# Neighbour maximum and graph attention on one core: the transposes of a step placed behind its second pick

## What is computed

```python
h = jnp.maximum(_layernorm(x), 0.0)
x = x + neighbour_max(h, adj)        # out[i, d] = max over j with adj[i, j] != 0 of h[j, d]
h = jnp.maximum(_layernorm(x), 0.0)
x = x + graph_attention(h, adj, W, a)  # masked softmax of leaky_relu(h W a1 + (h W a2)^T), times h W, elu
```

## Time and profile before

| | us |
|---|---|
| median of 3 runs | 768.66 (766.46 to 770.1) |
| the profiled execution | 767.11 |
| its span | 765.1 |
| TensorE busy | 699.9 (91%) |
| VectorE busy | 697.8 (91%) |
| ScalarE busy | 465.2 (61%) |
| GpSimd busy | 276.4 (36%) |

### The profile page before, as it was taken

How to read it: one execution, slowest core, us unless ns; L and a number is a source line. 1 busy time by engine, 2 the same in 40 slices (tenths; PEclk the granted TensorE clock), 3 DMA queues, 4 the chain that set the end, 5 groups by cost and what they waited for, 6 DMA issues and landing times.

```text
span 765.1 us, 14870 instructions
## 1 busy us (share of the span) xinstructions
PE 699.9 (91%) x5592; PEld 489.5 (64%) x5592; DVE 697.8 (91%) x1097; ACT 465.2 (61%) x682; POOL 276.4 (36%) x258
## 2 busy tenths in 40 slices
PE   1888999999999999999999999789999999999995
PEld 1344555555545555555555554489999999999995
DVE  9899889999999999999999999998998899899894
ACT  2878898888888889889889888363423121011000
POOL 0612033543543543543444534442330095043040
PEclk9999999999999999999999999899999999999998
DMA  9999768997777777877877754524433444543400
GB/s 306 305 372 383 278 220 270 281 309 265 254 238 253 264 232 249 274 234 239 273 244 231 274 167 147 183 84 131 132 132 111 165 141 176 179 147 143 175 20 17
DMA packets 62857, 162.55 MB, mean 212 GB/s; under 512 B 6400, under 2 KB 11136, under 8 KB 58688
## 3 DMA queue, kind: packets, MB, share of 16 engines
q1 hardware_dynamic: 53776, 138.75, 52.3%
q0 software_dynamic: 9008, 22.82, 11.0%
HBM read 117.51 MB, written 44.04 MB: 211 GB/s over the span
## 4 chain that ended last, share of the span: by engine, by line
PE 52%; ACT 18%; DVE 16%; issue 12%; DMA 1%; ACTq 0%; DVEq 0%; SPq 0%
PE pick_ps L702 22%; PE pick_ps L602 13%; ACT rest L401 7%; ACT depth L393 7%; DVE rest L1033 6%; DVE acc L855 5%; PE late_ps L574 5%; PE late_ps L615 4%; ACT edge_t L381 4%; PE order_ps L583 3%; PE late_ps L611 2%; PE late_ps L681 1%; DMA best<-x 1%; DVE acc L962 1%; PE late_ps L702 1%
## 5 line engine op out<-in xcount | busy, mean ns | idle before, releaser
L855 DVE TENSOR_TENSOR acc<-pick_ps,acc 128x1024 f32<-128x1024 f32 x248 | 302.5, 1220 | 32.9 <-PE pick_ps L602 30.4
L353 POOL DMA_INDIRECT found<-subset_max,entry x192 | 200.4, 1044 | 287.5 <-DVE entry L867 203.7
L1033 DVE SCALAR_TENSOR_TENSOR rest<-depth,curves_sb,stage 128x512 f32<-128x512 f32 x256 | 199.6, 820 | 14.7 <-PE pick_ps L702 2.3
L702 PE MATMUL pick_ps<-keys,rest 128*128 128x129 f32 x1792 | 207.1, 276 | 3.8 <-DVE rest L1033 3.8
L702 PEld LDWEIGHTS pick_ps<-keys,rest 128*128 128x128 f32 x1792 | 203.9, 192 | 7.9 <-DVE rest L1033 6.3
L392 ACT ACTIVATE first<-order_ps 128x1024 f16<-128x1024 f32 x128 | 132.4, 1035 | 64.2 <-PE order_ps L583 63.9
L393 ACT ACTIVATE depth<-order_ps 128x1024 f16<-128x1024 f32 x128 | 132.6, 1036 | 0.0
L574 PEld LDWEIGHTS late_ps<-ident_h,stage 128*128 128x128 f16 x1024 | 64.7, 100 | 84.5 <-ACT edge_t L381 53.0
L574 PE MATMUL late_ps<-ident_h,stage 128*128 128x128 f16 x1024 | 81.3, 224 | 37.5 <-ACT edge_t L381 24.4
L602 PE MATMUL pick_ps<-first,h_hi 128*128 128x512 f16 x256 | 97.8, 382 | 7.7 <-DVE acc L855 7.7
L602 PE MATMUL pick_ps<-second,h_hi 128*128 128x512 f16 x256 | 98.0, 383 | 2.3 <-DVE acc L855 2.3
(11 more groups left out here) (142 smaller groups left out, 682.0 us busy)
## 6 DMA issues: line engine op xcount, KB each, us to landing
stage<-adj SPq DMA_DIRECT2D x64, 1024.0 KB, 5.7
edge_units<-edge_t SPq DMA_DIRECT2D x64, 512.0 KB, 6.1
stage<-edge_units SPq DMA_DIRECT2D x32, 1024.0 KB, 4.8
subset_max<-keys POOLq DMA_DIRECT2D x12, 512.0 KB, 8.2
found<-subset_max,entry POOLq DMA_INDIRECT x192, 5.3
best<-x SPq DMA_DIRECT2D x4, 512.0 KB, 6.1
subset_max<-x POOLq DMA_DIRECT2D x4, 512.0 KB, 7.5
out<-keys POOLq DMA_DIRECT2D x7, 256.0 KB, 3.3
```

The costliest lines, as they stand in the source:

```text
L353: nc.gpsimd.indirect_dma_start(found[:, n % NG, s, :], None, subset_max, bass.IndirectOffsetOnAxis(entry[:, n, s:s + 1], 0)).then_inc(gath ...
L702: last = nc.tensor.matmul(out_ps(q, b), weight[:, n % WEIGHTS, b * P:(b + 1) * P], wh[:, c, :], start=c == 0 and starts(q, b), stop=c == C ...
L855: V.tensor_tensor(acc[:, q % 2, :], pick_ps[k][:, :], acc[:, q % 2, :], ALU.max).then_inc(raised, 1)
L1033: V.scalar_tensor_tensor(out=weight[:, n % WEIGHTS, :], in0=limit[:, q % 4, :], scalar=slope[:, c:c + 1], in1=units[:, m % EDGES, k * TI:( ...
```

## The change

In the queue of TensorE `flip(g + AHEAD)` moves from the place behind `rank(g + 3)` to the one behind `pick(g, 1)`, ahead of `digest`. No instruction, wait or count is added or removed, and no other queue is edited. In the last steps (from `g` = 123) there is no `flip`, and nothing differs.

```diff
@@ -715,8 +715,6 @@
                     pick(g, 0)
                     if g + 3 < PAIRS:
                         rank(g + 3)
-                    if g + AHEAD < PAIRS:
-                        flip(g + AHEAD)
                     if g == PAIRS - 4:
...
                     pick(g, 1)
+                    if g + AHEAD < PAIRS:
+                        flip(g + AHEAD)
                     if g >= 2:
                         digest(g // 2 - 1, g % 2)
```

## The result

| | before | after |
|---|---|---|
| median, us (range) | 769.38 (766.46 to 770.88) | 759.62 (758.07 to 760.85) |
| profiled execution (span) | 767.11 (765.1) | 758.9 (756.9) |
| TensorE, VectorE busy | 699.9, 697.8 | 698.5, 700.1 |

The ratio is 0.9877, with a 95% interval from 0.984 to 0.9914: the change saves 9.8 us. (The median of before is of four runs; the forecast started from three, 768.7.) The forecast was 741.7, a saving of 27, with a range of 736 to 756. The sign is right, the size is not, and 759.6 lies above the range.

What follows compares the result with a forecast made beforehand. The prediction took the turns' wait for the edge copy to bound the loop, with VectorE bounding it afterwards. Gains of 2.6, 23.0 and 1.7 us, less 0.3, gave 27.0: from the median of 768.7 to 741.7, range 736 to 756.

Steps and rivals of the forecast that it cites:

- What bounds the kernel: In the loop over `g`, dependencies closing every two steps, 7.11 us, through the wait of `flip` for the edge copy.
- the pick's leaving the loop: The second pick's four matmuls (0.86 us) leave the loop between edge copy and ranks; 6.25 us remain for two steps.
- the sum: Gains of 2.6 us (first five turns), 23.0 (other 49) and 1.7 (step 0), less 0.3 for handoffs: 27.0.
- Rival A: In the loop, VectorE sets the length after the change: 741.7 us, with 737 to 748; chance 76%.
- VectorE takes over at 53.06 to 53.15 for 16 steps: In the steady loop VectorE's own work sets the length, where 16 steps took 56.91 us; gain about 3.76.
- Step 0: VectorE's wait of 2.01 us for the second pick behind the turns goes, some 0.3 comes back: 1.7 gained.
- Bias matmul (C): The digest's bias matmul, waiting for ScalarE's key copy, inherits the turns' stall; only step 0 gains: 767 us; chance 6%.
- small matmuls (D): On TensorE, turns into digest, sixteen small matmuls in a run cost 0.34 us a step: 774 us; chance 6%.
- Rival B: A second loop of handoffs takes over; edge copy waits for turns or ScalarE's rank waits grow: 756 us; chance 12%.
- SyncE's and GpSimd's queues: Load and store come within 0.9 us of before, traffic rises to 264 GB/s, fetches keep 3 us cover: nothing lost.

## Why the prediction was wrong, step by step

**What bounds the kernel, and the pick's leaving the loop: right.** The 55 waits at the turns are gone, and the 0.86 of the second pick no longer stands between edge copy and ranks. With the fetches out of both kernels the change is worth 766.84 - 741.76 = 25.1 us; the sum said 27.0. (Rival A's low end is a slip: 768.7 - 31.0 is 737.7, not 737. Nothing hangs on it.)

**VectorE takes over at 53.06 to 53.15 for 16 steps: right but for a small term.** Without fetches it is 53.57 on average. Two takes directly behind each other cost 2.55 - 1.22 = 1.33 from start to start (the double rows at 388.58 and 389.34), as the second needs the first's `acc`. I had let a stop of 1.08 vanish to nothing; 0.11 of it stays. Four times 0.11 is 0.44 in 16 steps, which brings 53.06 to 53.50. Over 6.1 times 16 steps that is 2.7 us, enough for the difference of 25.1 and 27.0.

**Step 0: right in kind.** The changed kernel's second take follows the mask without a wait, and the next tile's first take comes at 89.00 instead of 90.15, 1.15 earlier where 1.7 was forecast:

```profile
28.85 1.44 DVE L844 TENSOR_SCALAR rest<-depth 128x2048 f16<-128x2048 f16 x1
30.21 1.22 DVE L855 TENSOR_TENSOR acc<-pick_ps,acc 128x1024 f32<-128x1024 f32 x1
```

**Bias matmul (C) and small matmuls (D): both rightly set aside.** The bias matmul at 389.30 stands 0.55 behind the turns of 388.75, where an undisturbed run of eight takes 0.45, and the waits view has no wait of it for the key copy. Turns and digest take 0.45 each (385.70, 386.15, 386.60), 0.056 a matmul, the second eight no slower than the first. The 81 ns that the Trainium skill (TensorE: Matmul & The Clock Gate, Back-to-back issue gap) gives for a lasting stream don't show in a run of sixteen.

**Rival B named a time near the result (756), but not its mechanism.** Of its signs neither came: from 60 to 490 us ScalarE's waits for ranks fell from 55.9 us to 44.4, and without fetches to 31.6, near the 0.5 a turn that was forecast, and its edge copy waits for turns once, 0.3 us. Without fetches all of the lateness went.

**SyncE's and GpSimd's queues: here the prediction failed.** I wrote that load and store "come within 0.9 us of where they were", that the traffic of 264 GB/s was under 379 shown elsewhere, and of the fetches "nothing lost". Each was costed alone: the load by its landing, the fetch by its cover, the traffic by its mean. None was held against the other. Those 0.9 us put the load behind the first fetch instead of beside it. The price was 17.9 - 2.5 = 15.4 us. It appears in a row that has no DMA in it: VectorE waiting for picks, 15.4 us against 1.6 without fetches. That 13.8 is most of the 17.9; the rest I didn't place. Over the changed-order kernels the order of their times follows these waits closely: 1.6 us at 741.8, 5.7 at 746.1, 9.5 to 10.7 at 752 to 754, 15.4 at 759.6, 18.1 at 762.3, 21.5 to 21.6 at 763.6 to 765.7 (an exception is 5.5 at 753.3). The GB/s behind the loads don't order the times so.

**What stays open.** That the fetches, by where they stand against the loads, make TensorE's signals late is shown by taking them away, by moving them and by bringing the meeting into the kernel before. How a DMA holds up TensorE's signals is not: whether it is the packets, or GpSimd's work of issuing them, no run here parts. The issuing alone is not enough, as the kernel before issues the same 192 fetches without one late signal until its loads move. Nor does the distance to the last fetch tell all: with the load one step later, loads 0.2 to 0.3 us behind a fetch had 230 to 279 GB/s, in the kernel before loads 0.05 behind one 332 to 366; and the kernel with the load one step later was the slowest of the changed order at a middling 274 GB/s.

## What to carry to other kernels

When an edit moves the wait that releases a DMA, lay the new issue time against those of the other DMA queues, fetches by index above all, and not only against the buffer that it fills: here a shift of 0.9 us went with a loss of 15.4 of 25.1 us of gain. If an engine waits for a producer whose own starts are on time, look at the DMA traffic of that moment before blaming the order of instructions. And try the order of a tight loop once with the side traffic taken out: the difference says whether to tune the loop or the traffic, and here moving six fetches by one or two takes gave back 13.5 of 17.9 us.

## What the runs showed of the hardware

- A matmul's signal can reach its waiters 0.9 us late while the starts on TensorE stay on time (pick at 386.60 to 387.24, take at 388.58 instead of 387.67), to ScalarE as to VectorE: the ranks of 370.25 released `first` at 371.45, 1.20 later, while in the kernel before it was 0.63 (ranks at 314.52, `first` at 315.15). Rows of the changed kernel, TensorE and ScalarE:

```profile
370.25 0.59 PE L583 MATMUL order_ps<-edge_t,order_w 128*128 128x512 f16 x2
```

```profile
371.45 1.02 ACT L392 ACTIVATE first<-order_ps 128x1024 f16<-128x1024 f32 x1 [1.20 <-PE order_ps L583]
```

- Only TensorE's signals were late. In the changed kernel, from 100 to 440 us, 109 of its 446 recorded ones came over 0.1 us late, of VectorE's and ScalarE's none of 599, and a take lasts 1.22 us as before. Every trace with late signals also lacks some records, so these counts are low bounds.
- From 1.5 to 5 us behind a load of 1 MB that was issued 0.3 to 1.2 us behind an indirect fetch of 128 rows, all DMA together moved 231 GB/s on average (154 loads), against 345 without a fetch near (83); 6 loads of the kernel before at that distance had 332.
- Packets of indirect fetches of 64 bytes an entry took as long as those of 512 (7.9% and 7.8% of 16 engines' span).
- Sixteen matmuls of 128 columns in a run keep 0.056 us each at the full clock (1.00 in the stretch table).
